# Selective scan: the step sizes' three terms summed by identity products on TensorE, and their product with u taken from PSUM tile by tile

## The chip, the cores and the metric

The kernel runs on one core of one Trainium2 chip. The metric is the device time of one execution in microseconds. The kernel is one program that computes a stack of eight layers; the change touches two of them, which share one function.

## The reference, cut to what matters

Layers one and seven of the stack are selective scans over four batches of 512 steps, with 512 channels (four tiles of 128 partitions) and 16 states. Cut to the recurrence:

```python
x = silu(xc + conv_b[None, :, None])                       # u
x_dbl = jnp.einsum('bdl,ed->bel', x, x_proj_w)
dt_low, Bm, Cm = jnp.split(x_dbl, [dt_rank, dt_rank + d_state], axis=1)
dt = jnp.einsum('brl,dr->bdl', dt_low, dt_proj_w)
dt = jax.nn.softplus(dt + dt_proj_b[None, :, None])        # the step sizes, delta
def step(state, inp):
    d, b, c, u = inp
    dA = jnp.exp(d[..., None] * A)
    state = state * dA + (d * u)[..., None] * b[:, None, :]
    y = jnp.einsum('bdn,bn->bd', state, c)
    return (state, y)
```

Everything is float32. The kernel computes softplus(v) as three terms: ln(1 + e) with e = exp(-|v|), the rounding error of 1 + e, which is e - ((1 + e) - 1), and max(v, 0).

## The kernel before, in words

Both scans are built by stage_mamba (L239 on). Each engine has its own list of instructions, written out in program order; semaphores tie the lists together. A batch is worked through in 32 units (index k): for each half h of the four channel tiles and each of the 16 states one unit, which scans two tiles along the 512 steps. In a unit

- ACT computes two tiles dA = exp(delta * A) (L652), in a ring of three PSUM banks,
- POOL computes dB = delta*u times the row of B, 128x1024 (L684), in a ring of four, and two units later the product of the second scanned tile with the row of C (L666),
- DVE runs the two scans (L745, L754) and the product of the first tile with C (L762). In units 5, 12, 21 and 28 DVE does the second product too (L768) and POOL none,
- PE adds both products into the PSUM banks of y by a matmul with the identity (L504, L512).

While batch b is scanned, the inputs of batch b + 1 are made ready between the units, at units set by a few constants (`PROJECT, TURN, CONV, XDBL, STEP` and `SILU, EXP, LOG, ERROR, ADD_ERROR, DELTA`), with ACT three units later than PE (LAG). PE writes all of this preparation into two PSUM banks (ps_w) in turn; an item may start when the item two before it (free_bank) has been copied out. The last steps of the preparation, called the handover here, are:

- units 16 to 19 on PE (19 to 22 on ACT): v for each tile (L484), |v| into delta (L598), max(v, 0) into positive (L600),
- ACT, unit 23 and 24: e = exp(-|v|) into xin (L606), ln(1 + e) into delta (L610), each over all four tiles,
- DVE, unit 24: the rounding error into du, two passes 128x2048 (log_error, L716 and L717),
- POOL, unit 26: delta += du (add_error, L660),
- DVE, unit 28: delta += positive (L722) and du = delta * u (L725), both 128x2048 (softplus).

In the first stage (m0) batch 0 is prepared ahead of the loop, and the last batch prepares batch 0 of the seventh layer (m3), which is parked in DRAM and loaded when m3 starts. So m0 has one handover ahead of the first scan and four in the loop, m3 has three. In batch 2 of m0, PE also turns the weights of the next layer (units 22 to 25, "reweigh", L454 to L458, copied by ACT three units later) and DVE builds its diagonal matrices (units 20 to 23, L699).

## Time and profile before

| | |
|---|---|
| median of 3 runs | 4247.79 us (4243.83 to 4247.87) |
| the profiled execution | 4247.61 us, span 4245.6 us |
| mean granted clock of TensorE | 0.923 |
| first scan stage, first to last scan | 77 to 585 us of the span |
| second scan stage, first to last scan | 3217 to 3708 us |

The profile is one execution on the chip. Times in its rows are microseconds from the start of the span. Matmuls overlap: a record lasts longer than the distance to the next. A matmul of f32 operands stands in it as two records. The other layers (624 to 3200 us and 3720 us on) hold none of the lines that change.

### The profile page before, as it was taken

To read this page: it belongs to the slowest core of one execution; us is meant where nothing else is said; L and a number is where in the kernel's file an instruction comes from. 1 tells how busy PE (TensorE), PEld (TensorE's weight loads), DVE (VectorE), ACT (ScalarE), POOL (GpSimd) and SP (SyncE) were. 2 spreads that over 40 slices of the span, in tenths; PEclk is the share of its full clock that TensorE was granted. 3 is DMA by queue.
4 is the path that set the end of the run, shared out by engine and by line. 5 is a ranking of instruction groups with operands and counts; after the bars stand their busy time and mean duration, and the time that the engine had idled before them with its cause. 6 is when DMAs were issued, how large, how long until landed. Compare 5 with 4: busy or idle time off the path is not lost. (4 is left out here: it accounts for less than half of the span.)

```text
span 4245.6 us, 46735 instructions
## 1 busy us (share of the span) xinstructions
PE 3610.5 (85%) x15184; PEld 1723.7 (41%) x15184; DVE 2977.1 (70%) x4169; ACT 1769.3 (42%) x2947; POOL 1500.1 (35%) x1038
## 2 busy tenths in 40 slices
PE   6888846999999999698999879785886777679898
PEld 2233323555555555342333344343332322244454
DVE  4899988578877774557888256527667999844663
ACT  4555532222222221243777453336664555421254
POOL 3898954112211120054000100003445999900122
PEclk8899977999999999797999989896998999989999
DMA  4455431132133302256775110002004554412320
GB/s 124 133 136 138 131 117 39 48 99 71 62 99 101 94 27 66 84 128 107 79 77 57 53 60 0 3 0 72 0 0 134 136 139 133 130 47 69 79 54 22
DMA packets 246858, 333.98 MB, mean 79 GB/s; under 512 B 43428, under 2 KB 145062, under 8 KB 245576
## 3 DMA queue, kind: packets, MB, share of 16 engines
q1 hardware_dynamic: 246648, 331.36, 31.6%
q8 instruction: 110, 1.80, 0.2%
q14 instruction: 100, 0.82, 0.1%
HBM read 280.17 MB, written 51.13 MB: 78 GB/s over the span
## 5 line engine op out<-in xcount | busy, mean ns | idle before, releaser
L652 ACT ACTIVATE m_dA<-m_delta,m_a_neg 128x512 f32<-128x512 f32 x512 | 350.0, 689 | 472.5 <-DVE m_H_bank L745 384.9
L504 PE MATMUL m_y<-m_H,ident 128*128 128x512 f32 x512 | 307.4, 689 | 186.4 <-DVE m_H L762 186.4
L1833 DVE TENSOR_REDUCE a_core_minus_max<-a_core_a 128x1 f32<-128x512 f32 x512 | 317.1, 684 | 59.1 <-PE a_core_a L1659 59.1
L684 POOL TENSOR_TENSOR m_dB<-m_du,m_BC 128x1024 f32<-128x1024 f32 x128 | 315.5, 2465 | 44.4 <-DMA m_BC<-bc_ready 35.7
L512 PE MATMUL m_y<-m_H,ident 128*128 128x512 f32 x512 | 294.2, 665 | 31.1 <-POOL m_H L666 30.9
L666 POOL TENSOR_TENSOR m_H<-m_H,m_BC 128x512 f32<-128x512 f32 x224 | 299.9, 1339 | 45.5 <-DVE m_H L754 43.9
L1785 ACT ACTIVATE X<-a_core_s 128x512 f32<-128x512 f32 x512 | 264.6, 603 | 94.5 <-PE a_core_s L1659 94.5
L684 POOL TENSOR_TENSOR XN<-m_du,m_BC 128x1024 f32<-128x1024 f32 x128 | 300.8, 2356 | 2.7 <-DMA m_BC<-bc_ready 2.7
L1225 POOL TENSOR_TENSOR ctxT<-ctxT,f_scales 128x1024 f32<-128x1024 f32 x48 | 104.2, 2171 | 532.4 <-DVE ctxT L1050 532.4
L1291 DVE SCALAR_TENSOR_TENSOR XN<-f_u,f_power_back,XN 128x512 f32<-128x512 f32 x128 | 95.8, 749 | 231.0 <-PE f_u L1122 231.0
L1185 ACT ACTIVATE XN<-f_g,f_power_back 128x512 f32<-128x512 f32 x128 | 88.0, 687 | 403.6 <-PE f_g L1122 403.5
L504 PEld LDWEIGHTS m_y<-m_H,ident 128*128 128x128 f32 x512 | 96.5, 209 | 370.4 <-DVE m_H L762 315.0
L1196 ACT CAST f_inter_high<-XN 128x512 fp32r<-128x512 f32 x128 | 79.5, 621 | 384.7 <-DVE XN L1291 384.7
L1659 PE MATMUL a_core_a<-a_core_k,a_core_q 96*128 96x512 bf16 x512 | 209.2, 411 | 25.7 <-ACT a_core_max_rows L1803 10.1
L1112 PE MATMUL f_acc<-f_wdown_high,f_inter_high 128*128 128x512 f32 x512 | 224.1, 438 | 0.0
L1233 POOL TENSOR_TENSOR XN<-f_mag,ctxT 128x1024 f32<-128x1024 f32 x48 | 127.7, 2660 | 215.2 <-DVE f_mag L1059 109.2
L1114 PE MATMUL f_acc<-f_wdown_high,f_inter_low 128*128 128x512 f32 x512 | 202.7, 396 | 0.0
L1113 PE MATMUL f_acc<-f_wdown_low,f_inter_high 128*128 128x512 f32 x512 | 202.2, 395 | 0.0
L1120 PE MATMUL f_g<-f_xn_high,f_wh 128*128 128x512 f16 x512 | 196.3, 383 | 1.4 <-ACT f_wh L1098 1.4
L1659 PE MATMUL a_core_s<-a_core_q,a_core_k 98*128 98x512 bf16 x512 | 192.0, 386 | 5.4 <-ACT X L1785 4.5
L1120 PE MATMUL f_u<-f_xn_high,f_wh 128*128 128x512 f16 x512 | 194.9, 381 | 1.4 <-ACT f_wh L1098 1.4
L745 DVE TENSOR_TENSOR_SCAN m_H_bank<-m_dA,XN 128x512 f32<-128x512 f32 x128 | 157.4, 1230 | 55.1 <-ACT m_dA L652 36.0
(411 smaller groups left out, 8395.3 us busy)
## 6 DMA issues: line engine op xcount, KB each, us to landing
m_BC<-bc_rows SPq DMA_DIRECT2D x224, 512.0 KB, 4.9
XN<-in_L_ffn_w_dram SPq DMA_DIRECT2D x72, 256.0 KB, 2.6
m_BC<-bc_ready SPq DMA_DIRECT2D x32, 512.0 KB, 4.9
ternary<-ctxT SPq DMA_DIRECT2D x96, 128.0 KB, 1.7
a_core_q<-a_q_parts SPq DMA_DIRECT2D x48, 256.0 KB, 13.0
a_core_k<-a_k_parts SPq DMA_DIRECT2D x48, 256.0 KB, 14.8
f_w_tern<-ternary SPq DMA_DIRECT2D x24, 512.0 KB, 5.9
f_core_q<-f_q_parts SPq DMA_DIRECT2D x24, 512.0 KB, 8.0
```

Source lines behind the costliest of these rows:

```text
L504: pe.matmul(ps_y[:, 0, :], ident[:], HD[n % NH], start=False, stop=True, skip_group_check=True).then_inc(s_ad, 1)
L512: pe.matmul(ps_y[:, 1, :], ident[:], HP[n % NH], start=False, stop=True, skip_group_check=True).then_inc(s_ap, 1)
L652: act.activation(dA[:, i % NA, :], delta[b % 2][:, e, :], ACT.Exp, scale=a_neg[:, e, k % N:k % N + 1]).then_inc(s_dA, 1)
L666: pool.tensor_tensor(HP[n % NH], HP[n % NH], BC[n % NS][:, 1, :], ALU.mult).then_inc(s_hp, 1)
L684: pool.tensor_tensor(dB[n % ND][:], du[b % 2][:, h * EH:(h + 1) * EH, :], BC[n % NS][:, 0:1, :].broadcast_to([P, EH, L]), ALU.mult).then_i ...
L1112: pe.matmul(ps_acc[:, t, :], high, DH[gb][:, q % 4, :], start=(q % 4 == 0), stop=False)
L1113: pe.matmul(ps_acc[:, t, :], high, DL[gb][:, q % 4, :], start=False, stop=False)
L1114: m = pe.matmul(ps_acc[:, t, :], low, DH[gb][:, q % 4, :], start=False, stop=(q % 4 == 3))
L1120: pe.matmul(out, w[0], xh[:, k, toks], start=(k == 0), stop=False)
L1659: pe_last = pe.matmul(out[:, cols], lhs(c, k), rhs(c, k), start=(c == 0), stop=(c == NCH - 1 and mask is None))
L1785: act.activation(prob[pair][e][:, j, q0:], ps_s[:, at % NR, q0:], ACT.Exp, scale=hs.scale).then_inc(s_exp, 1)
L1833: dve.tensor_reduce(mx[u % 2][:, qt, h:h + 1], ps_a[:, at % NR, 0:n], AX.X, ALU.max, negate=True).then_inc(s_red, 1)
```

## The change

It replaces the two additions and the product over all four tiles by a step per tile. At units 23 to 26 PE has a new item, "sum": three matmuls with the identity add delta, du and positive of one tile in a bank of ps_w. One unit later on DVE (24 to 27) the product with u is taken from that bank (times_u), and three units later on ACT (26 to 29) the bank is copied into delta (copy_sum), after DVE's product. Exp moves to unit 22, the logarithm and the rounding error to unit 23. The counts of the semaphores for delta and du go by tiles. The diff, cut to its core:

```diff
         PROJECT, TURN, CONV, XDBL, STEP = (0, 1, 2, 3), (5, 6, 11, 12), (7, 8, 9, 10), 13, (16, 17, 18, 19)
-        SILU, EXP, LOG, ERROR, ADD_ERROR, DELTA = (10, 13), 23, 24, 24, 26, 28
+        SILU, EXP, LOG, ERROR, SUM = (10, 13), 22, 23, 23, (23, 24, 25, 26)
         LAG = 3
...
             ITEMS += [("project", 0, e) for e in range(EB)] + [("conv", 0, e) for e in range(EB)]
-            ITEMS += [("xdbl", 0, 0)] + [("step", 0, e) for e in range(EB)]
+            ITEMS += [("xdbl", 0, 0)] + [("step", 0, e) for e in range(EB)] + [("sum", 0, e) for e in range(EB)]
         BEFORE = len(ITEMS)
...
                         here.append(("step", b + 1, STEP.index(k)))
+                    if k in SUM:
+                        here.append(("sum", b + 1, SUM.index(k)))
                 AT[b, k] = here
...
                 if b == B:
-                    sp.wait_ge(s_du, NB)
+                    sp.wait_ge(s_du, NB * EB)
+                    sp.wait_ge(s_del, NB * EB)
                     for i in range(3):
...
                     pe.wait_ge(s_relu, b * EB + i + 1)
+                elif kind == "sum":
+                    pe.wait_ge(s_del, b * EB + i + 1)
+                    pe.wait_ge(s_du, b * EB + i + 1)
                 else:
...
                     pe.matmul(out, dt_T[:, i * P:(i + 1) * P], xdbl[0:R, :], start=True, stop=True).then_inc(s_dt, 1)
+                elif kind == "sum":
+                    pe.wait_ge(s_relu, (b + 1) * EB)
+                    pe.wait_ge(s_ln, b + 1)
+                    pe.wait_ge(s_err, b + 1)
+                    pe.matmul(out, ident[:], delta[b % 2][:, i, :], start=True, stop=False)
+                    pe.matmul(out, ident[:], du[b % 2][:, i, :], start=False, stop=False)
+                    pe.matmul(out, ident[:], positive[:, i, :], start=False, stop=True).then_inc(s_sum, 1)
                 else:
...
                 if b >= 2:
-                    act.wait_ge(s_du, b - 1)
+                    act.wait_ge(s_du, (b - 1) * EB)
                     act.wait_ge(s_y0, EB * (b - 1))
...
                 if b:
-                    act.wait_ge(s_del, b)
+                    act.wait_ge(s_sum, b * EB)
                 act.activation(delta[b % 2][:, e, :], bank("step", b, e), ACT.Abs,
...
                 act.activation(delta[b % 2][:], xin[:, :, TAPS - 1:], ACT.Ln, bias=1.0).then_inc(s_ln, 1)
+
+            def copy_sum(b, e):
+                act.wait_ge(s_sum, b * EB + e + 1)
+                act.wait_ge(s_du, b * EB + e + 1)
+                act.copy(delta[b % 2][:, e, :], bank("sum", b, e)).then_inc(s_del, 1)
 
...
                 norm.root(act)
+                for e in range(EB):
+                    copy_sum(0, e)
             for b in range(B):
-                act.wait_ge(s_del, b + 1)
+                act.wait_ge(s_del, (b + 1) * EB)
                 for k in range(NU):
...
                             log_part(b + 1)
+                        if k - LAG in SUM:
+                            copy_sum(b + 1, SUM.index(k - LAG))
                     for j in range(EH):
...
         def _(pool):
-            def add_error(b):
-                pool.wait_ge(s_ln, b + 1)
-                pool.wait_ge(s_err, b + 1)
-                pool.tensor_tensor(delta[b % 2][:], delta[b % 2][:], du[b % 2][:], ALU.add).then_inc(s_log, 1)
-
             def product(n):
...
 
-            if given:
-                pool.sem_inc(s_log, 1)
-            else:
-                add_error(0)
             for b in range(B):
                 for k in range(NU):
-                    if b + 1 < NB:
-                        if k == ADD_ERROR:
-                            add_error(b + 1)
                     n, h = b * NU + k, k // N
-                    pool.wait_ge(s_du, b + 1)
+                    pool.wait_ge(s_du, b * EB + (h + 1) * EH)
                     if b < FIRST and k % N == 0:
...
 
-            def softplus(b):
-                dve.wait_ge(s_log, b + 1)
-                dve.wait_ge(s_relu, (b + 1) * EB)
-                dve.tensor_tensor(delta[b % 2][:], delta[b % 2][:], positive, ALU.add).then_inc(s_del, 1)
-                dve.wait_ge(s_del, b + 1)
-                dve.wait_ge(s_u, (b + 1) * EB)
-                dve.tensor_tensor(du[b % 2][:], delta[b % 2][:], u[b % 2][:], ALU.mult).then_inc(s_du, 1)
+            def times_u(b, e):
+                dve.wait_ge(s_sum, b * EB + e + 1)
+                dve.wait_ge(s_u, b * EB + e + 1)
+                dve.tensor_tensor(du[b % 2][:, e, :], bank("sum", b, e), u[b % 2][:, e, :], ALU.mult).then_inc(s_du, 1)
 
...
                 norm.inverse(dve)
-                softplus(0)
+                for e in range(EB):
+                    times_u(0, e)
             for b in range(B):
...
                             log_error(b + 1)
-                        if k == DELTA:
-                            softplus(b + 1)
+                        if k - 1 in SUM:
+                            times_u(b + 1, SUM.index(k - 1))
                     n = b * NU + k
```

PE in batch 0 of m0, after the change, from the matmuls that add unit 22 to y on (m_y are the adds into y, m_w the two banks of the preparation):

```order
L525 MATMUL m_y<-m_H,ident 128x512
L517 MATMUL m_y<-m_H,ident 128x512
L495 MATMUL m_w<-m_delta,ident 128x512
L496 MATMUL m_w<-m_du,ident 128x512
L497 MATMUL m_w<-XN,ident 128x512
L525 MATMUL m_y<-m_H,ident 128x512
L517 MATMUL m_y<-m_H,ident 128x512
L495 MATMUL m_w<-m_delta,ident 128x512
L496 MATMUL m_w<-m_du,ident 128x512
L497 MATMUL m_w<-XN,ident 128x512
```

Before the change only the two adds of each unit (L512, L504) stood there in turn, with nothing between them. A sum stands ahead of the add of DVE's product of its own unit.

DVE at the same place, before:

```order
L762 TENSOR_TENSOR m_H<-m_H_bank,m_BC 128x512
L716 TENSOR_SCALAR m_du<-m_xin 128x2048
L717 TENSOR_TENSOR m_du<-m_xin,m_du 128x2048
...
L762 TENSOR_TENSOR m_H<-m_H_bank,m_BC 128x512
L722 TENSOR_TENSOR m_delta<-m_delta,XN 128x2048
L725 TENSOR_TENSOR m_du<-m_delta,m_u 128x2048
```

and after:

```order
L726 TENSOR_SCALAR m_du<-m_xin 128x2048
L727 TENSOR_TENSOR m_du<-m_xin,m_du 128x2048
L752 SCALAR_TENSOR_TENSOR m_H_bank<-m_dA,XN 128x512
L761 SCALAR_TENSOR_TENSOR m_H<-m_dA,XN 128x512
L769 TENSOR_TENSOR m_H<-m_H_bank,m_BC 128x512
L732 TENSOR_TENSOR m_du<-m_w,m_u 128x512
L752 SCALAR_TENSOR_TENSOR m_H_bank<-m_dA,m_dB 128x512
L761 SCALAR_TENSOR_TENSOR m_H<-m_dA,m_dB 128x512
L769 TENSOR_TENSOR m_H<-m_H_bank,m_BC 128x512
L732 TENSOR_TENSOR m_du<-m_w,m_u 128x512
```

The two 128x2048 passes behind the fourth unit are gone, and a 128x512 product reading m_w stands behind each of four units.

PE in batch 2 of m0, after the change, where the next layer's weights are turned (L460, L462) in the same two banks:

```order
L460 MATMUL m_w<-ident,m_in_rows 128x128 x4
L525 MATMUL m_y<-m_H,ident 128x512
L517 MATMUL m_y<-m_H,ident 128x512
L460 MATMUL m_w<-ident,m_in_rows 128x128 x4
L495 MATMUL m_w<-m_delta,ident 128x512
L496 MATMUL m_w<-m_du,ident 128x512
L497 MATMUL m_w<-XN,ident 128x512
L525 MATMUL m_y<-m_H,ident 128x512
L517 MATMUL m_y<-m_H,ident 128x512
L462 MATMUL m_w<-ident,m_x_rows 128x48 x4
L495 MATMUL m_w<-m_delta,ident 128x512
```

Each sum now has a turn of the weights ahead of it, so the turn two items before a sum used the sum's bank.

## Rows read from the trace of the kernel before

**Rows 1.** The page, part 5: line engine op out<-in xcount | busy, mean ns | idle before, releaser.

```profile
L652 ACT ACTIVATE m_dA<-m_delta,m_a_neg 128x512 f32<-128x512 f32 x512 | 350.0, 689 | 472.5 <-DVE m_H_bank L745 384.9
```

**Rows 2.** A stretch of the first scan stage: busy us (xinstructions) by engine, PEclk, DMA share, GB/s.

```profile
185.00:300.00 115.00, 97.43 (x206) 37.76 (x206) 102.74 (x105) 63.80 (x89) 107.46 (x57) 0.90 0.58 144
```

**Rows 3.** Timeline of DVE, first handover: start, us, line, out<-in, idle before.

```profile
163.19 3.22 DVE L716 TENSOR_SCALAR m_du<-m_xin 128x2048 f32<-128x2048 f32 x1
166.45 2.29 DVE L717 TENSOR_TENSOR m_du<-m_xin,m_du 128x2048 f32<-128x2048 f32 x1
168.66 1.22 DVE L745 TENSOR_TENSOR_SCAN m_H_bank<-m_dA,m_dB 128x512 f32<-128x512 f32 x1
...
170.91 0.67 DVE L762 TENSOR_TENSOR m_H<-m_H_bank,m_BC 128x512 f32<-128x512 f32 x1
171.77 1.23 DVE L745 TENSOR_TENSOR_SCAN m_H_bank<-m_dA,m_dB 128x512 f32<-128x512 f32 x1 [0.20 <-ACT m_dA L652]
...
175.74 1.23 DVE L745 TENSOR_TENSOR_SCAN m_H_bank<-m_dA,XN 128x512 f32<-128x512 f32 x1 [1.04 <-POOL XN L684]
...
179.26 1.23 DVE L745 TENSOR_TENSOR_SCAN m_H_bank<-m_dA,XN 128x512 f32<-128x512 f32 x1 [0.60 <-POOL XN L684]
...
182.10 2.81 DVE L722 TENSOR_TENSOR m_delta<-m_delta,XN 128x2048 f32<-128x2048 f32 x1
184.94 3.23 DVE L725 TENSOR_TENSOR m_du<-m_delta,m_u 128x2048 f32<-128x2048 f32 x1
188.10 1.22 DVE L745 TENSOR_TENSOR_SCAN m_H_bank<-m_dA,m_dB 128x512 f32<-128x512 f32 x1
```

**Rows 4.** Timeline of POOL, the same stretch.

```profile
161.75 2.35 POOL L684 TENSOR_TENSOR m_dB<-m_du,m_BC 128x1024 f32<-128x1024 f32 x1
164.07 1.26 POOL L666 TENSOR_TENSOR m_H<-m_H,m_BC 128x512 f32<-128x512 f32 x1
168.89 4.50 POOL L660 TENSOR_TENSOR m_delta<-m_delta,m_du 128x2048 f32<-128x2048 f32 x1 [3.56 <-DVE m_du L717]
```

**Rows 5.** Single lines of code: duration ns min/median/max, first and last start, forms.

```profile
L504 PE MATMUL m_y<-m_H,ident x512: 592/592/1222, 80.5 to 3708.8; 128*128 128x512 f32 x171
...
L716 DVE TENSOR_SCALAR m_du<-m_xin x8: 1218/2934/3248, 62.2 to 3560.1; 128x2048 f32<-128x2048 f32 x8
...
L732 DVE TENSOR_TENSOR XN<-XN,m_y x32: 677/679/689, 139.7 to 3711.1; 128x512 f32<-128x512 f32 x32
...
L566 ACT COPY m_xin<-m_w x32: 577/578/588, 27.5 to 3491.1; 128x512 f32<-128x512 f32 x32
...
L454 PE MATMUL m_w<-ident,m_in_rows x16: 418/421/477, 416.3 to 3223.3; 128*128 128x128 f32 x16
```

**Rows 6.** Timeline of PE behind the first rounding error.

```profile
171.63 2.07 PE L504 MATMUL m_y<-m_H,ident 128*128 128x512 f32 x2 [5.68 <-DVE m_H L762]
...
175.04 1.02 PE L504 MATMUL m_y<-m_H,ident 128*128 128x512 f32 x2
```

**Rows 7.** PE by stretches: busy us (xinstructions), granted clock, DMA share, GB/s.

```profile
172.00:174.00 2.00, 2.00 (x3) 0.50 0.00 0
...
296.00:298.00 2.00, 0.78 (x2) 0.94 0.05 18
```

**Rows 8.** Timeline of DVE in batch 2 of the first stage.

```profile
398.60 5.41 DVE L699 TENSOR_SCALAR m_taps<-ident,m_next_small 128x128 f32<-128x128 f32 x4
```

**Rows 9.** Timeline of POOL at the same place.

```profile
401.00 2.33 POOL L684 TENSOR_TENSOR XN<-m_du,m_BC 128x1024 f32<-128x1024 f32 x1
```

**Rows 10.** Timeline of all engines ahead of the first scan.

```profile
57.54 6.02 PE L464 MATMUL m_w<-ctxT,m_in_T 128*128 128x512 f32 x8
...
63.43 2.29 DVE L717 TENSOR_TENSOR m_du<-m_xin,m_du 128x2048 f32<-128x2048 f32 x1
...
67.00 1.28 ACT L652 ACT_TABLE_LOAD   x1
...
77.47 1.23 DVE L745 TENSOR_TENSOR_SCAN m_H_bank<-m_dA,m_dB 128x512 f32<-128x512 f32 x1 [2.45 <-POOL m_dB L684]
```

10 lines of the change are left out of this document (5 added, 5 removed).

## The prediction

> **What bounds the kernel now.** The page's costliest group, the dA of the scans (0.69 us each), belongs to the two scan stages that the change touches [rows 1]; its busy shares run over the whole span and say nothing of them. The table by stretches tells what is tight there: in one batch of the first stage DVE is busy 102.7 of 115 us, POOL 107.5, PE 97.4, ACT 63.8 [rows 2]; the second stage runs the same loop. DVE's timeline shows that it walks its list almost without a hole: a unit is scan, scan, product, and 3.11 us later the next one [rows 3]. So DVE sets the pace; POOL and PE have little to spare.
>
> Once in each batch DVE does the handover of the step sizes for the next batch. I read it in the first one [rows 3]: the rounding error (L716, L717) takes from 163.19 to 168.66, 5.47 us; then four units; then the two 128x2048 passes L722 and L725, 182.10 to 188.10, 6.00 us. Two of the four units begin late, by 1.04 and 0.60 us, on a dB tile of POOL, because POOL has spent 4.50 us on the first sum (L660) [rows 4]. From the end of the error (E) to unit 28 that is 188.10 - 168.66 = 19.44 us. There are eight handovers: one ahead of the first scan, seven inside the loops (four and three).
>
> **What the change does to one handover.** It removes L660 from POOL and L722 and L725 from DVE. It adds to PE three identity products per tile, to DVE one product 128x512 out of PSUM, to ACT one copy. Exp, logarithm and error stand one unit earlier, so after E come units 23 to 26, with a product behind each; the counterpart of the 19.44 us is E to unit 27.
>
> DVE alone would gain. A product with one operand in PSUM costs 0.68 us [rows 5], four are 2.7 us for the 6.00 us removed, and the 1.24 us of late dB go too. But each product must wait for its sum, and PE pays for it. An identity product 128x512 in f32 is two records in the trace: at the full clock two take 1.02 us and one lasts 0.59, so they start 0.43 apart; at the half level two take 2.07, one 1.22, so 0.85 apart [rows 5, 6]. A sum is six records: 2.58 us at the full clock. PE's own work for a unit, two adds into y, is four records, 1.72 us. Together 4.30 us in a unit that lasts 3.11 + 0.68 = 3.79 us on DVE: **for these units PE becomes the bound.**
>
> And it starts slow. PE stands idle during the error, before and after the change, and on its return at 171.63 it runs at the half level: granted 0.50 at 172 to 174, four records in the first 3.41 us, and full from 175.04 on [rows 6, 7]. I take five half records and one full for the first sum, 4.68 us. With 0.1 us for the start and 0.16 us for the landing (0.59 less 0.43) it is there at E + 4.95. DVE, through with unit 23 at 2.25 + 0.67 = E + 2.9 [rows 3], waits 2.0 us. From there the sums land every 4.30 us: 9.25, 13.55, 17.85. The last product ends at 18.5: unit 27 at **E + 18.5, against 19.44, 0.9 us gained.** ACT's copy (0.58 us, [rows 5]) of the first sum comes after the first scan of unit 24 and one dA, done at about E + 8.1; PE asks for its bank at the third sum, at 9.1 + 1.7 = E + 10.8: nothing. SP's loads are not moved past anything; the parking at the end of the first stage waits for eight semaphore counts instead of one, with units still to run: nothing.
>
> **The error itself gets longer.** Before, POOL stood blocked ahead of L660 during it, which let DVE in. L716 asked at 163.19, while POOL was in dB (to 164.07); it lasted 3.22 us and ended at 166.41, thus began to work only when the next POOL operation, from 164.07 to 165.3, was over as well. A short L699, also tensor_scalar, shows the same: four of them took 5.41 us, until the third POOL operation in a row ended at 403.3 [rows 4, 8, 9]. So tensor_scalar waits until POOL has a hole. Now nothing blocks POOL there: at the start of the error, one unit earlier, it still has the rest of a dB, a product (1.26) and a dB (2.35) to do before it must wait for unit 23. That is 2.8 us if POOL is as far ahead as its ring lets it, 3.7 us if it lags as in the first batch. With 1.22 and 2.21 us for the two passes the error takes 6.2 to 7.15 us; I take 6.7. Before, the six ordinary handovers averaged 5.15 us (L716 at its shortest, median and longest: [rows 5]). So 1.55 us lost, and an ordinary handover costs 1.55 - 0.9 = **+0.65 us, times six +3.9 us.**
>
> Here the Trainium skill speaks otherwise. "SBUF — State Buffer", in its part on the two sides of SBUF, says of the shared port pair: whichever of the two engines starts first gets it for the whole instruction, and the other blocks. By that L716 would wait for the one operation in progress only; this trace, with 3.22 us where one operation left 0.9 us, disagrees. What the sum would be by the rule is rival B.
>
> **The third handover of the first stage** is different: in units 22 to 25 PE also turns the next layer's weights, in the same two banks. The second listing of the change shows it: each sum now stands two places behind such a turn and must wait until ACT has copied it, and ACT does that three units late in its own order, only after the first scan of the very unit whose product waits for the sum. That closes a ring, per unit: scan 1.23, dA 0.69, copy 0.58, four transposes of the next weights about 0.7 (0.42 each, overlapped, [rows 5]), sum and landing 2.74, product 0.68: 6.6 us. First sum at 1.23 + 0.69 + 0.58 + 4.84 = E + 7.35, the next at 14.0 and 20.6, the last, with no turn before it, at 26.5, unit 27 at E + 27.2 instead of 19.44: 7.8 us lost. The error there stands right behind the L699 of the same unit, which already wait for POOL's hole, so it takes 3.5 us (before 4.2). Together **+7.1 us.**
>
> **The handover ahead of the first scan.** L717 ends at 65.7, the first scan starts at 77.47 [rows 10]. What PE did during that time (eight records of the next projection, from 57.54) now stands behind the sums, so PE comes to them after 8 us idle, at the half level. Sums landed: 65.8 + 4.68, then 2.58 each: 78.4; product 0.68, copy 0.58; then ACT loads the table of Exp, which in the old order lay under the wait, 1.28, and dA 0.69: first scan at 81.6. **+4.1 us.** If the clock were still full it would be +2.1.
>
> **Sum.** 3.9 + 7.1 + 4.1 = 15.1 us on the profiled execution's own 4247.61 us (span 4245.6), which is the median of the three times to 0.2 us: **4263 us.** A measurement of this kernel tells about 0.2%, 8.5 us, from no change.
>
> **Rivals.**
> - **A, as above**, 0.62. For it: the half clock after the idle stretch and the long tensor_scalar both stand in the rows, and PE's 4.30 against DVE's 3.79 us holds at any clock.
> - **B, DVE gets the port after one operation**, 0.16. The lagging case is then 0.17 + 1.22, POOL's product 1.23, 2.21: 4.8 us, 0.3 less than before. An ordinary handover gains 1.25 us, six 7.5; the other two remain: +3.7, **4251 us**, no change. For it: L716 at its shortest, 1.22 us. Against: five of seven took 2.9 us or more.
> - **C, port at once and clock kept, faster**, 0.12. PE is idle from about 0.9 us after the start of the error. If the error takes only 4.8 us, PE returns after 4 us instead of 6, and may still run full: in the second handover PE came back at about 297 after 4.8 us of idleness, and the clock granted at 296 to 298 was still 0.94 [rows 7]. Then the first sum lands at E + 2.85, before DVE asks at 2.9; the rest by PE's 4.30, unit 27 at 16.4. An ordinary handover gains 3.0 + 0.3, six 20 us; the third of the first stage loses 5.0, the first handover 2.1: -13, **4234 us**. It decides at the point where a first sum takes less than DVE's 2.9 us. Against it: all restarts I looked at fell to half at or soon after the first record.
> - **D, the half level lasts over the second sum too**, 0.10. Four adds at 0.85 and a second sum at 5.1 instead of 2.58 are 4.2 us more in each ordinary handover: some 25 us more, **4288 us**. Against: with sums added PE is denser than where it recovered after 3.4 us.
> That POOL's relief would help later is no case of its own: DVE waits for POOL rarely outside the handover, and the two waits inside are in the sum.
>
> **The numbers.** 4263 is A. A's own bounds: error 6.2 to 7.15 (3 us down or up), one half record more or less per handover (0.43 times seven, 3 us), the ring of the third handover 6 to 7.2 us per unit (2 us): 4255 to 4271 if these fall together, and some microseconds more for a stage that answers with waits of its own. To hold 8 in 10 the range takes in B and a part of D: **4244 to 4281**. Within 0.2% (4239.3 to 4256.3): B and the lowest fifth of A, 0.28; faster: C, 0.12; slower 0.60.
>
> **What would show it.** Right: the wait of the product out of PSUM for the third matmul of the sum, about 2 us at the first and 0.5 to 1 us at each later tile, in every handover; the error longer than 6 us with POOL busy through its first half; granted clock 0.5 at the first sum; 6.6 us per unit in the third handover; the first scan near 81.6 us. Wrong: L716 at 1.2 to 2 us (B), no wait for the first sum (C), half clock in the second sum (D), or waits of DVE for ACT's copies, which I cost at nothing.

## The result, and the profile after

| | kernel before | changed kernel |
|---|---|---|
| median of 13 runs each, same chip | 4243.14 us (4237.74 to 4247.87) | 4252.0 us (4242.93 to 4258.42) |
| ratio, 95% interval | | 1.0023 (1.0014 to 1.0031) |
| the profiled execution | 4247.61 us, span 4245.6 us | 4252.0 us, span 4250.3 us |
| mean granted clock of TensorE | 0.923 | 0.928 |

The change makes the kernel slower by some 9 us. I had forecast slower, by 15.1 us, at 4263 us; the range of 4244 to 4281 us holds the measured 4252.0. The mechanism came as forecast; the size did not.

The first handover of the changed kernel in DVE's timeline answers to [rows 3]. Columns: start, us, engine, line, out<-in, idle before and its releaser.

```profile
161.59 5.17 DVE L726 TENSOR_SCALAR m_du<-m_xin 128x2048 f32<-128x2048 f32 x1
166.79 2.29 DVE L727 TENSOR_TENSOR m_du<-m_xin,m_du 128x2048 f32<-128x2048 f32 x1
169.00 1.23 DVE L752 TENSOR_TENSOR_SCAN m_H_bank<-m_dA,XN 128x512 f32<-128x512 f32 x1
...
173.79 0.69 DVE L732 TENSOR_TENSOR m_du<-m_w,m_u 128x512 f32<-128x512 f32 x1 [1.87 <-PE m_w L497]
...
178.08 0.69 DVE L732 TENSOR_TENSOR m_du<-m_w,m_u 128x512 f32<-128x512 f32 x1 [0.78 <-PE m_w L497]
...
182.37 0.69 DVE L732 TENSOR_TENSOR m_du<-m_w,m_u 128x512 f32<-128x512 f32 x1 [0.78 <-PE m_w L497]
...
186.66 0.69 DVE L732 TENSOR_TENSOR m_du<-m_w,m_u 128x512 f32<-128x512 f32 x1 [0.77 <-PE m_w L497]
187.27 1.22 DVE L752 TENSOR_TENSOR_SCAN m_H_bank<-m_dA,XN 128x512 f32<-128x512 f32 x1
```

The rounding error goes from 161.59 to 169.00: 7.41 us, where it took 5.47. Then the two losses of PE stand in brackets: 1.87 us for the first sum, 0.78 for each later one, and the products are 4.29 us apart. Unit 27 starts at E + 18.27 (187.27 - 169.00).

POOL's timeline at the same place says why the error is long; it answers to [rows 4].

```profile
159.80 2.35 POOL L694 TENSOR_TENSOR m_dB<-m_du,m_BC 128x1024 f32<-128x1024 f32 x1
162.12 1.26 POOL L683 TENSOR_TENSOR m_H<-m_H,m_BC 128x512 f32<-128x512 f32 x1
163.34 2.33 POOL L694 TENSOR_TENSOR m_dB<-m_du,m_BC 128x1024 f32<-128x1024 f32 x1
171.41 1.27 POOL L683 TENSOR_TENSOR m_H<-m_H,m_BC 128x512 f32<-128x512 f32 x1 [5.74 <-DVE m_H L761]
```

L726 asks at 161.59 and needs 1.21 us by itself. It ends at 166.76, so it began its own work at 165.55: when the third operation, ending at 165.67, was over, to 0.1 us. Two of the three (162.12 and 163.34) began after it had asked. All six ordinary handovers of this trace look like this: the line's median is 4848 ns.

```profile
L726 DVE TENSOR_SCALAR m_du<-m_xin x8: 1214/4848/5170, 60.2 to 3561.7; 128x2048 f32<-128x2048 f32 x8
```

PE by stretches of 2 us (busy, matmuls, granted clock, DMA share, GB/s) answers to [rows 7]:

```profile
168.00:170.00 2.00, 0.77 (x1) 0.50 0.00 0
170.00:172.00 2.00, 2.00 (x4) 0.50 0.00 0
172.00:174.00 2.00, 2.00 (x5) 0.83 0.06 19
174.00:176.00 2.00, 2.00 (x6) 1.00 0.69 164
```

The first sum runs at the half level (0.50, that is 1.2 GHz) and the clock is back at its full level within the third stretch: as forecast, only the first sum pays (in the second handover a little more does: the first sum comes 2.81 us late there, the second 0.99). In the stretch that answers to [rows 2], PE went up to 99.19 us of 115, POOL down from 107.46 to 101.55:

```profile
185.00:300.00 115.00, 99.19 (x218) 39.68 (x217) 102.27 (x106) 64.18 (x90) 101.55 (x56) 0.91 0.53 145
```

The third handover of the first stage, DVE's timeline:

```profile
425.31 1.21 DVE L726 TENSOR_SCALAR m_du<-m_xin 128x2048 f32<-128x2048 f32 x1
426.56 2.29 DVE L727 TENSOR_TENSOR m_du<-m_xin,m_du 128x2048 f32<-128x2048 f32 x1
...
436.24 0.69 DVE L732 TENSOR_TENSOR m_du<-m_w,m_u 128x512 f32<-128x512 f32 x1 [4.56 <-PE m_w L497]
...
442.72 0.69 DVE L732 TENSOR_TENSOR m_du<-m_w,m_u 128x512 f32<-128x512 f32 x1 [2.97 <-PE m_w L497]
...
448.94 0.69 DVE L732 TENSOR_TENSOR m_du<-m_w,m_u 128x512 f32<-128x512 f32 x1 [2.70 <-PE m_w L497]
...
454.93 0.69 DVE L732 TENSOR_TENSOR m_du<-m_w,m_u 128x512 f32<-128x512 f32 x1 [2.48 <-PE m_w L497]
```

The products are 6.48, 6.22 and 5.99 us apart. PE's timeline names the ring: it waits for ACT's copy of the turned weights before it may turn the next ones.

```profile
439.36 0.45 PE L462 MATMUL m_w<-ident,m_x_rows 48*128 48x48 f32 x4 [1.44 <-ACT m_in_T L568]
439.84 1.12 PE L495 MATMUL m_w<-m_delta,ident 128*128 128x512 f32 x2
```

**The balance.** I add up two pairs of traces by stages (the pair above, and one trace of each kernel in the first set of experiments) and give the mean of the two. A handover is measured from unit 22 to unit 28, which both kernels have.

| stretch | predicted | measured, changed less before |
|---|---|---|
| six ordinary handovers | +3.9 | +5.8 |
| third handover of the first stage | +7.1 | +6.8 |
| end of the error to the first scan | +4.1 | +4.7 |
| behind unit 28 of batch 0 | 0 | -1.5 |
| the other parts of both scan loops | 0 | -2.5 |
| layers between the scan stages | 0 | -5.2 |
| from the start to the end of the first error | 0 | -3.1 |
| entry of the second scan stage, and all behind it | 0 | +0.2 |
| sum | +15.1 | +5.1, as the spans |

(The rows are rounded; they add up to the spans.) So what I had worked out is there, and 2 us larger (17.3). Twelve microseconds are missing in places where the change does nothing, or where I expected nothing of it. Part of that is the choice of the traces: the two of the kernel before come from executions 4.5 and 2.6 us above their medians, the two of the changed kernel from executions 0 and 2.3 us below, together 4.7 us per pair. The medians differ by 9 to 10 us, which leaves 7 to 8 us to be found. The last two sets of experiments look for them.

### The profile page after: what moved, and what is told of

Read it like the earlier page. It is cut to its first block and busy times, and to the rows that moved or that the text cites. A ratio compares the mean times of both kernels' runs of the same rounds, so it can differ in the third digit from the quotient of the medians.

```text
span 4250.3 us, 47228 instructions
## 1 busy us (share of the span) xinstructions
PE 3654.2 (86%) x15328; PEld 1756.8 (41%) x15376; DVE 2958.1 (70%) x4185; ACT 1782.8 (42%) x2979; POOL 1438.5 (34%) x1030
## 3 DMA queue, kind: packets, MB, share of 16 engines
q8 instruction: 112, 1.84, 0.2%
## 5 line engine op out<-in xcount | busy, mean ns | idle before, releaser
L517 PE MATMUL m_y<-m_H,ident 128*128 128x512 f32 x512 | 292.7, 659 | 124.0 <-DVE m_H L769 123.9
L694 POOL TENSOR_TENSOR m_dB<-m_du,m_BC 128x1024 f32<-128x1024 f32 x128 | 301.4, 2355 | 107.3 <-DVE m_du L732 70.0
L683 POOL TENSOR_TENSOR m_H<-m_H,m_BC 128x512 f32<-128x512 f32 x224 | 284.9, 1272 | 144.0 <-DVE m_H L761 143.7
L525 PE MATMUL m_y<-m_H,ident 128*128 128x512 f32 x512 | 273.3, 623 | 1.5 <-POOL m_H L683 1.4
L1129 PE MATMUL f_u<-f_xn_low,f_wh 128*128 128x512 f16 x512 | 195.0, 381 | 0.0
```

The lines of the kernel that those rows point to most:

```text
L517: pe.matmul(ps_y[:, 0, :], ident[:], HD[n % NH], start=False, stop=True, skip_group_check=True).then_inc(s_ad, 1)
L525: pe.matmul(ps_y[:, 1, :], ident[:], HP[n % NH], start=False, stop=True, skip_group_check=True).then_inc(s_ap, 1)
L683: pool.tensor_tensor(HP[n % NH], HP[n % NH], BC[n % NS][:, 1, :], ALU.mult).then_inc(s_hp, 1)
L694: pool.tensor_tensor(dB[n % ND][:], du[b % 2][:, h * EH:(h + 1) * EH, :], BC[n % NS][:, 0:1, :].broadcast_to([P, EH, L]), ALU.mult).then_i ...
```

## The experiments

Times differ a little between chips, so each is set against the kernel before in its own set (4241.91, 4243.87, 4241.18 and 4243.68 us). Of these four sets the changed kernel ran in the first alone; where a run of another set is held against it, its +10.4 us stands for it. A median's distance is good to some 4 or 5 us, and for c3 and c4, with five executions each, to some 6:

| run | us | against before | ratio, 95% interval |
|---|---|---|---|
| changed kernel again | 4252.31 | +10.4 | 1.0024 (1.0015 to 1.0033) |
| a3 POOL held | 4238.63 | -3.3 | 0.9993 (0.9984 to 1.0002) |
| a4 turn apart | 4244.54 | +2.6 | 1.0003 (0.9994 to 1.0012) |
| b1 early, POOL free | 4255.54 | +11.7 | 1.0029 (1.0017 to 1.0042) |
| b2 early, POOL blocked | 4241.43 | -2.4 | 0.9999 (0.999 to 1.0008) |
| b3 error last | 4245.33 | +1.5 | 1.0004 (0.9995 to 1.0013) |
| b4 two terms | 4229.39 | -14.5 | 0.997 (0.9959 to 0.9981) |
| c1 clock kept | 4245.69 | +4.5 | 1.0009 (1.0 to 1.0018) |
| c2 POOL's pass back | 4252.7 | +11.5 | 1.0025 (1.0015 to 1.0035) |
| c3 three mends | 4212.33 | -28.9 | 0.993 (0.9917 to 0.9944) |
| c4 four mends | 4211.05 | -30.1 | 0.9927 (0.9914 to 0.9941) |
| d1 before, loads later | 4243.54 | -0.1 | 0.9999 (0.999 to 1.0008) |
| d2 changed, loads later | 4254.65 | +11.0 | 1.0029 (1.0019 to 1.004) |
| d3 before, layout | 4244.11 | +0.4 | 1.0004 (0.9995 to 1.0013) |
| d4 changed, layout | 4256.45 | +12.8 | 1.0034 (1.0022 to 1.0046) |

**Both kernels again** (no edit; the kernel before in one execution, the changed kernel in eleven).

> The kernel before, looked at once more. Between the end of the first scan stage and the start of the second no line differs between the two kernels, and yet the changed one needed 6.3 us less there in its profile. If that is chance, this trace differs from the first one of the same kernel by some microseconds there too; if the change acts on those stages, the two traces of before agree within 1 us.

> The changed kernel, measured beside the following ones on one chip: 8 to 10 us above before. Its handovers as in its first trace: error 7.4 us, first sum 1.9 us late, the others 0.8 us, unit 27 at 18.3 us after the end of the error, 26.8 in batch 2 of the first stage.

The kernel before gave 4244.53 us, the changed kernel 4252.31. Their traces repeat the pattern: errors of 7.39, 7.06 and 7.05 us in the changed kernel's first stage, first waits of 2.52, 1.86 and 2.04 us. They are the second pair of the balance.

**Is it POOL that holds the tensor_scalar? Hold POOL (a3).** The theory: L726 waits until POOL's run of operations ends. Rival: the moved error is long for another reason. POOL gets a wait that puts a hole beside the error.

```diff
+                    if b + 1 < NB and k == ERROR + 2:
+                        pool.wait_ge(s_err, b + 2)
                     n, h = b * NU + k, k // N
```

> POOL waits for the rounding error ahead of the dB of unit 25, as it did ahead of its own sum before the change. Theory A (tensor_scalar gets the port only in a hole of POOL's work): L726 starts one dB (2.35 us) earlier, the error takes 4.9 to 5.1 us instead of 7.4 in six handovers, the dB of unit 25 is late for nobody, 12 to 14 us less than the changed kernel. Rival (L726 is long for another reason, its length does not hang on what POOL has to do next): L726 stays at 4.8 to 5.2 us and the time stays; or POOL's dB comes late and DVE waits for it in unit 25 or 26 by what the error gains.

It took 13.7 us less than the changed kernel beside it. L728 is the tensor_scalar here; DVE and, below it, POOL:

```profile
164.00 2.82 DVE L728 TENSOR_SCALAR m_du<-m_xin 128x2048 f32<-128x2048 f32 x1
```

```profile
162.18 2.34 POOL L696 TENSOR_TENSOR m_dB<-m_du,m_BC 128x1024 f32<-128x1024 f32 x1
164.48 1.25 POOL L683 TENSOR_TENSOR m_H<-m_H,m_BC 128x512 f32<-128x512 f32 x1
169.23 2.34 POOL L696 TENSOR_TENSOR m_dB<-m_du,m_BC 128x1024 f32<-128x1024 f32 x1 [3.49 <-DVE m_du L729]
```

It still sits out one whole operation that starts after it asked (164.48 to 165.73) and then needs its 1.1 us. The errors fall to 5.07, 4.76 and 4.79 us in the ordinary handovers of the first stage (the third stays at 3.46). But the first waits for a sum grow, from 1.87 to 2.81 us in the first handover: here all of the first sum runs at the half level, although PE had been idle for less time (3.79 us against 6.09). The second handover of the changed kernel shows the same 2.81 us, after 5.12 us of idle time.

**Move the error alone (b1, b2).** Both are the kernel before, with exp, logarithm and error a unit earlier; in b1 POOL's addition stays at unit 26 and so leaves POOL free during the error, in b2 it moves too and blocks POOL there.

```diff
-            SILU, EXP, LOG, ERROR, ADD_ERROR, DELTA = (10, 13), 23, 24, 24, 26, 28
+            SILU, EXP, LOG, ERROR, ADD_ERROR, DELTA = (10, 13), 22, 23, 23, 26, 28
```

(b2: the last two are 25 and 27.)

> The kernel before, with Exp, logarithm and error one unit earlier as in the change, but POOL's sum left at unit 26 and DVE's two passes at 28. No sum on TensorE. POOL is then not blocked while DVE computes the error. Theory A (the port comes free for tensor_scalar only in a hole of POOL's work): the error takes 7.1 to 7.4 us instead of 5.2 to 5.5 in six handovers, 10 to 14 us more than before in all. Rival (what lengthens it in the change is the work of the sums themselves): 5.2 to 5.5 us, time as before.

> As b1, with POOL's sum and DVE's passes one unit earlier too (25 and 27), so that POOL is blocked during the error as before. Theory A: error 5.2 to 5.5 us again, time within 4 us of before. Rival (units 22 and 23 are a worse place for the error, ACT or the second product of unit 21 being in the way): slower than before by 5 us or more.

b1 has no sum on PE and no product out of PSUM, and is 11.7 us slower; b2, with errors of 4.77 to 5.07 us, is level with the kernel before. The line of b1 is the changed kernel's, almost to the digit:

```profile
L716 DVE TENSOR_SCALAR m_du<-m_xin x8: 1214/4828/5147, 58.3 to 3560.3; 128x2048 f32<-128x2048 f32 x8
```

So moving the error out of the place where POOL stands blocked costs as much by itself as the whole change does. That the two are equal is partly chance. By the traces b1's six ordinary handovers cost 12.6 us more than before, its third and the start of the first scan nothing. The changed kernel's six cost 5.8 more, its third 6.8 and the start of the first scan 4.7, from which the missing twelve come off.

One handover of b1, the second, behaves otherwise. DVE, then POOL:

```profile
284.92 1.93 DVE L716 TENSOR_SCALAR m_du<-m_xin 128x2048 f32<-128x2048 f32 x1
286.89 4.31 DVE L717 TENSOR_TENSOR m_du<-m_xin,m_du 128x2048 f32<-128x2048 f32 x1
```

```profile
284.50 1.27 POOL L666 TENSOR_TENSOR m_H<-m_H,m_BC 128x512 f32<-128x512 f32 x1 [0.23 <-DMA m_BC<-bc_rows]
285.72 3.33 POOL L684 TENSOR_TENSOR m_dB<-m_du,m_BC 128x1024 f32<-128x1024 f32 x1
```

Here the tensor_scalar got in after the one operation in progress, POOL's dB took 3.33 us in place of 2.35, and then L717 took 4.31 in place of 2.29. b4 has the same in its second handover, and in the second handover of the kernel before (289.84) L716 took 1.22 us while the POOL operation that began with it took 2.35 in place of 1.26. So the two engines shut each other out in either direction. Over all 18 traces there are 126 handovers inside the loops. In 104 tensor_scalar sat out at least one operation that began after it asked. In 18, the third ones of the first stage, POOL had nothing ready behind what was in progress. In four (one each of the kernel before, b1, b4 and d3) it got in ahead of a POOL operation that was ready. What decides is open.

**The ring in the third handover (a4).** The turns of the next weights leave the sums' units.

```diff
-REWEIGH = {(2, 22 + i): (i,) for i in range(4)} if then
+REWEIGH = {(2, 14): (0,), (2, 15): (1,), (2, 20): (2,), (2, 21): (3,)} if then
```

> The next layer's weights are turned in units 14, 15, 20 and 21 of batch 2 instead of 22 to 25, so no turn stands between the sums. Theory (a ring from the first scan over dA, the copy of the turn and the sum to the product): the third handover of the first stage becomes like the others, unit 27 at 18.3 us after the end of the error instead of 26.8, and 7 to 8 us less than the changed kernel. Rival (the diagonal matrices of units 20 to 23 and the clock make it slow): it stays near 26 us.

7.8 us less than the changed kernel. The products of that handover now wait as elsewhere, and it is 8.4 us shorter (31.09 against 39.54 us).

```profile
436.14 0.69 DVE L732 TENSOR_TENSOR m_du<-m_w,m_u 128x512 f32<-128x512 f32 x1 [1.75 <-PE m_w L497]
440.43 0.69 DVE L732 TENSOR_TENSOR m_du<-m_w,m_u 128x512 f32<-128x512 f32 x1 [0.78 <-PE m_w L497]
444.73 0.69 DVE L732 TENSOR_TENSOR m_du<-m_w,m_u 128x512 f32<-128x512 f32 x1 [0.78 <-PE m_w L497]
449.02 0.69 DVE L732 TENSOR_TENSOR m_du<-m_w,m_u 128x512 f32<-128x512 f32 x1 [0.78 <-PE m_w L497]
```

**What does PE's part cost? (b3, b4, c1.)** b3 adds the terms in another order, so that two of the three products run during the error:

```diff
-                    pe.wait_ge(s_err, b + 1)
                     pe.matmul(out, ident[:], delta[b % 2][:, i, :], start=True, stop=False)
-                    pe.matmul(out, ident[:], du[b % 2][:, i, :], start=False, stop=False)
-                    pe.matmul(out, ident[:], positive[:, i, :], start=False, stop=True).then_inc(s_sum, 1)
+                    pe.matmul(out, ident[:], positive[:, i, :], start=False, stop=False)
+                    pe.wait_ge(s_err, b + 1)
+                    pe.matmul(out, ident[:], du[b % 2][:, i, :], start=False, stop=True).then_inc(s_sum, 1)
```

> The changed kernel with the order of the three terms turned: delta and positive first, then the wait for the error, then its product. Two of three products run while DVE computes the error. Theory (the first wait is the six records after the error at the half level): the first product's wait goes from 1.9 to about 0, the later ones (PE 4.30 us a unit against 3.79 on DVE) stay at 0.5 to 0.8; 10 to 14 us less than the changed kernel. Rival (the wait is the clock or the semaphore, not the amount of work): it stays above 1 us.

b4 leaves the rounding error's term out of the sum (it computes ln(1 + e) + max(v, 0) alone), so a sum is four records instead of six:

```diff
-                    pe.matmul(out, ident[:], du[b % 2][:, i, :], start=False, stop=False)
```

> The changed kernel with the term of the rounding error left out of the sum (it is computed, and waited for, but not added), so a sum is four records instead of six. Theory (PE's 1.72 + 2.58 us per unit against DVE's 3.79 makes the later waits): PE needs 3.44 us per unit, the waits at the second to fourth sum vanish and the first falls by about 1 us; unit 27 at 15.5 to 16.5 us after the error instead of 18.3, 20 to 24 us less than the changed kernel in all. Rival (a fixed delay of the hand-over between engines): the later waits stay at 0.8.

c1 has PE work during the error: four identity products more, whose result is overwritten, into the bank of the first sum.

```diff
+                    if b and i == 0:
+                        for _ in range(4):
+                            pe.matmul(out, ident[:], positive[:, 0, :], start=True, stop=True)
```

> The changed kernel with four more products with the identity in front of the first sum of each handover in the loops, into the same bank, which the sum then overwrites; they run while DVE computes the error, so TensorE stands idle for less than it does now. Theory (the first sum is late by its six records at the half level after idleness): the first wait falls from 1.9 us to 0 to 1 us, granted clock above 0.9 in the sum; 5 to 12 us less than the changed kernel. Rival (the first sum is late for another reason, or the clock falls all the same): the wait stays at 1.7 to 2.8 us, time as the changed kernel.

Against the changed kernel b3 gains 8.9 us (10 to 14 expected), b4 24.9 and c1 5.9. In b3's first handover the first wait is gone, the second is 0.95 us and the others stay at 0.78; its third handover gains nothing (40.05 us). In b4's first handover the first wait is 1.04 us and the later ones are gone: the products are 3.43 us apart, which is what PE's eight records per unit take (8 x 0.43) and what DVE needs by itself. My 3.79 us for DVE was too much: it held DVE's wait for dA of 0.20 us, and the 0.08 us by which each record laps over the next. PE sets the 4.30 in either case. In c1 the clock is at its full level when the error ends:

```profile
170.00:172.00 2.00, 0.75 (x3) 1.00 0.01 4
172.00:174.00 2.00, 2.00 (x6) 1.00 0.00 0
```

```profile
174.60 0.69 DVE L735 TENSOR_TENSOR m_du<-m_w,m_u 128x512 f32<-128x512 f32 x1 [0.17 <-PE m_w L500]
```

The first wait falls from 1.87 to 0.17 us, and to 0.17 in all six ordinary handovers, where it was 2.10 on average: the half level after PE's idle time costs 1.7 us here and 1.9 on average. In the third handover the first wait rises to 8.2 us (from 4.56), as the extra products lie on the ring there, so only 5.9 us of some 12 are left.

**Does POOL's relief bring the missing time? (c2.)** The changed kernel, with a pass 128x2048 (xin + xin into xin, read by nobody) on POOL at unit 26, where the addition stood.

> The changed kernel with a POOL pass 128x2048 put back at unit 26 (over xin, whose values are no longer needed), as long as the one removed. If the 4 us that the changed kernel wins back outside the handovers come from POOL's relief, they are lost again: the stretches outside the handovers take 775 us in all instead of 771, and the time rises by 4 to 6 us, with DVE waiting for dB after the handover. If not, the stretches stay at 771 us.

11.5 us above its kernel before, where the changed kernel stood 10.4 above: no difference. The scans wait for POOL for 3.4 us in all, as without the pass; before, it was 19.5 us, of which the handovers' late dB ([rows 3] hold those of the first, 1.04 and 0.60) make 11 us. Of the other 5 us that went, 4.3 are two single waits, of the first scan of all (2.45 us, now none) and of the first unit of batch 1 (2.41, now 0.55). So the relief gives nothing outside the handovers: that entry of my sum was rightly zero, and the missing time lies elsewhere.

**All mends together (c3, c4).** c3 is the changed kernel with the hole for POOL (a3), the turns apart (a4) and the error's term last (b3). c4 has besides, ahead of the first scan, the old handover (POOL's addition and two passes on DVE).

> The mends of a3, a4 and b3 together: POOL waits for the error ahead of the dB of unit 25, the weights are turned in units 14, 15, 20 and 21, and the term of the error is added last. If the three costs are separate, 13.7 + 7.8 + 7.0 us below the changed kernel: about 4224 us, 0.4% below before. If the first two products of a sum no longer fit into the shorter error (4.9 us instead of 7.4), the first wait comes back by up to 2 us and it is about 4232 us.

> As c3, and the handover ahead of the first scan is done as before the change (one pass on POOL, two on DVE). The sums cost 4 to 5.5 us there by the traces so far, so the first scan starts 11.8 us after the error instead of 15.7 to 17.3: 4 to 5 us below c3, about 4219 us. Rival (the table load or the start of the loop eats it): as c3.

c3 gains 39.3 us on the changed kernel, and beats the kernel before by 28.9 (some 17 expected). The single mends add up to 30.4 (13.7 + 7.8 + 8.9), so they help each other. The seven handovers in the loops say so more sharply than the medians: they are 42 us shorter in c3's trace, and 11, 9 and 10 us shorter in those of a3, a4 and b3. Its timelines show how, DVE first:

```profile
163.79 2.85 DVE L728 TENSOR_SCALAR m_du<-m_xin 128x2048 f32<-128x2048 f32 x1
166.67 2.29 DVE L729 TENSOR_TENSOR m_du<-m_xin,m_du 128x2048 f32<-128x2048 f32 x1
...
171.71 0.68 DVE L734 TENSOR_TENSOR m_du<-m_w,m_u 128x512 f32<-128x512 f32 x1
...
175.59 0.69 DVE L734 TENSOR_TENSOR m_du<-m_w,m_u 128x512 f32<-128x512 f32 x1 [0.37 <-PE m_w L497]
```

```profile
165.02 1.91 PE L494 MATMUL m_w<-m_delta,ident 128*128 128x512 f32 x2
166.73 1.73 PE L495 MATMUL m_w<-XN,ident 128*128 128x512 f32 x2
169.02 1.12 PE L497 MATMUL m_w<-m_du,ident 128*128 128x512 f32 x2 [0.56 <-DVE m_du L729]
169.98 1.02 PE L525 MATMUL m_y<-m_H,ident 128*128 128x512 f32 x2
```

In b3 the two early products also brought the clock up (0.98 at 168 to 170), but the error there lasted until 171.1, PE stood idle again for 2.85 us, and the clock was back at 0.50 at 172 to 174. With the short error PE waits 0.56 us and stays at its full level. A handover then takes 26.6 to 26.9 us from unit 22 to unit 28, against 31.3 to 32.5 in the changed kernel and 29.8 to 30.9 before; the third takes 26.7 (39.7, 32.8).

c4 starts its first scan 3.7 us earlier behind the error (11.86 against 15.60), but its median is only 1.3 us lower. With five executions each, scattered over 9 us, the medians cannot tell 1.3 from 3.7. The trace shows that part of the gain is taken back in one row of DVE, at the first unit of batch 1:

```profile
200.81 1.23 DVE L757 TENSOR_TENSOR_SCAN m_H_bank<-m_dA,m_dB 128x512 f32<-128x512 f32 x1 [3.04 <-POOL m_dB L699]
```

The same wait is 0.55 us in the changed kernel and 2.41 in the kernel before. It is the -1.5 us of the balance.

**Where does the wait at the first unit of batch 1 come from? (d1, d2.)** POOL waits there for its row of B and C, not for an engine. SP's queue, before the change (start, us, queue, line):

```profile
186.51 0.47 SPq L391 DMA_DIRECT2D bc_rows<-m_xdbl  x1
191.10 0.38 SPq L109 DMA_DIRECT2D m_next_a_in<-in_L_xattn_A_log_dram  x1
...
195.36 17.13 SPq L373 DMA_DIRECT2D m_BC<-bc_rows  x6
```

SP stores the rows, waits for them to land (4.6 us), issues eight loads for the next layer and only then the load that POOL waits for: POOL's dB starts at 201.43. That chain has its own pace, so a slower handover in front of it hides a part of the wait. Both kernels, with the eight loads issued behind the first 16 units of batch 1:

```diff
-                if then and b == 1:
-                    sp.wait_ge(s_wt, 1)
-                    nxt.load_small(sp)
-                    nxt.load_rows(sp)
                 for k in range(NS if b < FIRST else 0, NU):
+                    if then and b == 1 and k == 16:
+                        sp.wait_ge(s_wt, 1)
+                        nxt.load_small(sp)
+                        nxt.load_rows(sp)
```

> The kernel before, with SP's loads of the next layer's weights (eight transfers) issued behind the loads of the first 16 units of batch 1 of the first stage, not ahead of all of them. Open is where the changed kernel regains about 4 us in the loops outside the handover. Theory: in the kernel before the first unit of batch 1 waits 2.4 us for a dB, because POOL waits for that unit's row of B, which SP can load only behind the store of the rows and these eight issues (4.3 us); this queue has its own time, so a slower handover ahead of it hides a part of the wait. Then the wait is gone here, behind unit 28 of batch 0 it takes 13.5 to 13.9 us instead of 15.0 to 15.7, and the time falls by 1 to 2.5 us. Rival, the 4 us are scatter of the rings between DVE, ACT and POOL: no change there.

> The changed kernel with the same move of the loads. Theory: only 0.5 us are left to gain there, so the time is 0 to 0.5 us below the changed kernel's and the difference of this pair is 1.5 to 2 us larger than that of the two kernels, +10.5 to +12 us. Rival: the same difference as without it, 9 to 10 us.

The wait is gone: behind unit 28 of batch 0 the kernel before now needs 13.50 us (15.71 and 15.04). Yet the time did not fall. In SP's queue the eight loads now stand ahead of the row of unit 16 (242.53 to 248.32 in d1), and POOL stands idle ahead of the dB of that unit:

```profile
254.97 2.35 POOL L684 TENSOR_TENSOR m_dB<-m_du,m_BC 128x1024 f32<-128x1024 f32 x1 [2.14 <-issue]
```

From unit 16 to unit 23 the dB are then ready only 0 to 1.5 us ahead of their scans, against 2.6 to 4.0 in the kernel before. So POOL, being late, still has a dB and a product to do when the tensor_scalar of the same batch's handover asks: it takes 5.08 us instead of 2.95 or 1.22, its error 7.33 us. The expected 1 to 2.5 us were given back, by the same mechanism that the whole case turns on, but through the new place of the loads and not because a wait was gone. In the changed kernel the corresponding error grew from 7.10 to 9.20 us. The difference of the pair is 11.1 us, within the 10.5 to 12 that the theory asked, but the intervals of this pair and of the others overlap widely. Both errors grew, so this pair does not measure the hidden wait cleanly. What it shows is that the wait came from SP's queue.

**Is it where the program's instructions lie? (d3, d4.)** Both kernels, with the first memset and the first Exp of each scan stage cut in pieces, the arithmetic the same:

```diff
-            act.activation(a_neg[:], a_in[:], ACT.Exp).then_inc(s_a, 1)
+            for i in range(16):
+                part = (slice(None), i // 4, slice(i % 4 * 4, i % 4 * 4 + 4))
+                m = act.activation(a_neg[part], a_in[part], ACT.Exp)
+            m.then_inc(s_a, 1)
...
-            dve.memset(xin[:, :, 0:TAPS - 1], 0.0).then_inc(s_pad, 1)
+            for i in range(EB * (TAPS - 1)):
+                m = dve.memset(xin[:, i // (TAPS - 1), i % (TAPS - 1):i % (TAPS - 1) + 1], 0.0)
+            m.then_inc(s_pad, 1)
```

> The kernel before, with the same arithmetic but the first memset of each scan stage cut in 12 and the first Exp in 16 instructions, far from everything that is timed here: the instruction streams of DVE and ACT shift by 11 and 15 places. Theory that the 5 us by which the untouched layers differ are chance of where the program's instructions lie: the layers between the scan stages come out elsewhere than 2605 to 2607 us, perhaps 2598 to 2603, and the sum of the loops outside the handovers elsewhere than 775. Rival, that they come from the change itself: 2603 to 2607 us and 775 as before; the whole within 2 us of the kernel before, the cut instructions costing up to 2 us.

> The changed kernel with the same cut of the first instructions. By chance of where the instructions lie: untouched layers anywhere from 2598 to 2607 us, and the difference to its own pair 4 to 15 us. By the rival: 2600 to 2601 us, the loops outside the handovers 771, and the difference to its pair 9 to 10 us.

The kernel before hardly moved (+0.4 us); its layers between the scan stages took 2604.3 us, the rest of its loops 775.0. The changed kernel took 4256.45 us, 4.1 to 4.5 more than in its own two sets, the layers between 2604.3 instead of 2600.8 us and the rest of the loops 774.4 instead of 771. The rows that bound those layers in the changed kernel, first as it is, then cut (the first instruction of the next layer on DVE, and the first of the second scan stage):

```profile
604.95 0.06 DVE L186 MEMSET f_xnT_norm_eps<- 128x1 f32 x1 [1.46 <-PEq L76]
...
3205.78 0.07 DVE L704 MEMSET m_xin<- 128x12 f32 x1 [1.45 <-PEq L76]
```

```profile
607.87 0.06 DVE L186 MEMSET f_xnT_norm_eps<- 128x1 f32 x1 [1.46 <-PEq L76]
...
3212.14 0.37 DVE L708 MEMSET m_xin<- 128x1 f32 x12 [1.44 <-PEq L76]
```

In this pair the handovers cost 13.5 us more, the stretch from the error to the first scan 4.2, behind unit 28 of batch 0 1.1 less, the other parts of the loops 0.5 more, the layers between nothing, all the rest 0.4 more: +17.5 us, and the two profiled executions differ by 17.6 (4261.68 and 4244.11; the former is the highest of its six, and the medians differ by 12.3). So the 5.2 us in untouched layers need not come with the change: after a cut of instructions that lies elsewhere they are gone, 3.5 on the changed kernel's side and 1.7 on the other. But it is one trace of each, and where the instructions lie is not shown to be the cause. Over all 18 traces these layers take 2597.4 to 2607.1 us, with no edit in them. The six traces without sums on PE average 2604.8 us there (2602.9 to 2607.1), the twelve with them 2601.4 (2597.4 to 2604.3). A part of the difference may therefore go with the change after all; no run separates the two.

## Why the prediction was right or wrong

- **PE becomes the bound of the four units**: right. The later sums come every 4.29 us (predicted 4.30), the waits are 0.78 us. b4 shows the other side: with four records the waits vanish.
- **Half clock in the first sum only**: right. 0.50 there, first wait 1.87 us (predicted 2.0); c1 removes it. Rival D, half clock in the second sum too, did not come.
- **E to unit 27**: predicted 18.5 us, measured 18.54 on average of the six ordinary handovers (18.24 to 19.43). The gain of 0.9 us stands.
- **The error gets longer**: right in kind, short in size. The six ordinary ones average 7.20 us, just above my bounds of 6.2 to 7.15 (I took 6.7): POOL was the whole 3.6 to 4.0 us behind in every one. That makes an ordinary handover +1.13 us in this pair (+0.96 in the mean of two) and not +0.65. This is the one of the three terms that was clearly mis-sized, +5.8 us for +3.9. Rival B, the port after one operation, fell for the changed kernel: all six of its ordinary handovers sat out two operations that began after the tensor_scalar had asked. It came in single handovers of b1 and b4. The Trainium skill says in "SBUF — State Buffer", on the two sides of SBUF, that whichever starts first has the pair for the whole instruction and the other blocks. As I read it, the wait would end with the operation in progress, at 162.15; it ended at 165.67.
- **The third handover**: right. E to unit 27 took 26.77 us (predicted 27.2), the error 3.46 (3.5); a4 shows the ring to be the cause.
- **Ahead of the first scan**: right, 15.65 us and 17.23 from the end of the error (predicted 15.9). That the first scan came at 79.42 and not near 81.6 is only that the error ended 2 us earlier in this execution, ahead of anything changed.
- **The step that failed**: the sum. It put the rest of the program at nothing, for POOL's relief with a reason and for all else without one, and added 3.9 + 7.1 + 4.1 = 15.1 us to a single execution's 4247.61 us. The measured change is 8.9 us. The three terms came to 17.3 us in the traces, so they were not too large; what was put at nothing measured -12.1. Of that, 1.5 us are what SP's chain at the start of batch 1 takes in (DVE's wait of 2.41 us there was in the trace of before, and I had not asked what a later arrival would do to it). Some 5 us are the choice of the traces, and some 6 us lie in the other stretches, most of them without an edit, between the scan stages above all; the cause of these stays open. The pair d3 and d4, with the same change, differs by 12.3 us instead of 9 to 10. The base failed too: the median of 13 runs of that kernel is 4243.14, so 4.5 us of the distance between 4263 and 4252.0 are the base, the other 6.5 the size. A's own bounds were 4255 to 4271, and 4252.0 lies below them: it is in the range only because that was widened to take in B, which did not come in the changed kernel. That is luck.
- **C, faster**, failed as weighed: every first sum of the changed kernel was waited for, 1.84 us or more. But its condition was the right one. Where the first sum is ready before DVE asks, and the turns are out of the way, as in c3, the form gains 28.9 us on the kernel before (where POOL's hold, which also shortens the errors from 7.2 to 4.9 us, has its part).

What stays open: what decides how long the untouched layers take; when tensor_scalar gets in ahead of POOL's next operation; and why the whole first sum is slow in a3 and in one handover of the changed kernel, after a shorter idle time than elsewhere.

## What to carry to other kernels

Look at what another engine is doing at the new place before you move an instruction: here a tensor_scalar moved by one unit, out of a pause of POOL, cost as much as the whole change. The work moved to PE paid here when its late operand came last in the accumulation and PE wasn't let idle ahead of it; these two mends with the third handover's brought 39 us together where they brought 30 singly. And a forecast of some 0.3% needs the median of many runs for its base, and has to leave a few microseconds of either sign for layers that nobody touched. Ask too whether a wait of the old trace will take in a later arrival.

## What the runs showed of the hardware

- A tensor_scalar 128x2048 that takes 1.21 us alone waited for two POOL operations that began after it had asked in the changed kernel (5.17 us), for three in one handover of d2 (6.96 us), and for one in a3 (2.82 us). In single handovers it got in first, and POOL's operation was the one that waited (3.33 us in place of 2.35 in b1). So the trace agrees with the rule cited above in that the engines exclude each other; who comes next when both are ready it does not settle.
- Two early products raised TensorE's clock to its full level, and 2.85 us of idle time later it ran at half again (b3); with 0.56 us of idle time it stayed (c3).
- Eight loads issued at unit 16 instead of ahead of unit 0 came with an idle time of POOL of 2.14 us there, and POOL was late from then on: a tensor_scalar behind unit 23 took 5.08 us instead of 2.95 or less (d1), and the gain at unit 0 was gone.
- Layers with no edit in them take up to 10 us more or less (2597.4 to 2607.1 us) from one kernel and execution to another.
